# Causal convolution moved to TensorE, second scan direction prepared beside the first rows, local branch added up in DRAM

## The reference

```python
xn = rmsnorm(x)                                   # over channels
u, z = split(xn @ in_proj.T)
u = silu(causal_conv4(u) + conv1d_b)              # depthwise, 4 taps, per direction
dt, Bm, Cm = split(u @ x_proj.T)
delta = softplus(dt @ dt_proj.T + dt_proj_b)
h = exp(delta * A) * h + (delta * u) * Bm         # scan over 1024 tokens, 16 states
y = sum_n(h * Cm) + u * D
mamba = (y * silu(z)) @ out_proj.T
x1 = x + res_scale * (scale_mod * (mamba(xn) + flip(mamba(flip(xn))))
                      + sigmoid(conv3x3(xn) + dw_b) * xn)
x2 = x1 + attention(layernorm(x1))                # 6 heads of 64, causal
out = x2 + mlp(layernorm(x2))                     # 384 -> 1536 -> 384, gelu
```

## Time and profile before

| what | us |
|---|---|
| median of 3 runs | 4690.36 (4688.07 to 4693.26) |
| profiled execution | 4690.52 |
| its span | 4688.3 |
| VectorE busy | 4013.4 (86%) |
| TensorE busy | 3251.8 (69%) |
| POOL busy | 2847.9 (61%) |
| ACT busy | 2447.6 (52%) |

### The profile page before, as it was taken

How to read it: one execution, slowest core, us unless ns; L and a number is a source line. 1 busy time by engine, 2 the same in 40 slices (tenths; PEclk the granted TensorE clock), 3 DMA queues, 4 the chain that set the end, 5 groups by cost and what they waited for, 6 DMA issues and landing times.

```text
span 4688.3 us, 38816 instructions
## 1 busy us (share of the span) xinstructions
PE 3251.8 (69%) x10858; PEld 1667.3 (36%) x10858; DVE 4013.4 (86%) x2961; ACT 2447.6 (52%) x3430; POOL 2847.9 (61%) x1671
## 2 busy tenths in 40 slices
PE   4100677767777768777677777877687776777797
PEld 1000235512354224532255223542245322552372
DVE  5999899989898999989999898988989899998221
ACT  3433446555464555655466544656556554665262
POOL 2798467764676647765577646766477655776100
PEclk8555778877888878878788778888788877888898
DMA  2799469982788639885599828886388855988100
GB/s 85 181 248 246 103 144 206 216 210 77 186 197 216 163 101 207 201 216 131 133 207 207 211 80 188 199 217 167 98 200 200 216 147 123 206 201 186 51 6 14
DMA packets 223126, 772.34 MB, mean 165 GB/s; under 512 B 24666, under 2 KB 40330, under 8 KB 222890
## 3 DMA queue, kind: packets, MB, share of 16 engines
q0 software_dynamic: 110592, 402.70, 44.2%
q1 hardware_dynamic: 112298, 366.90, 24.4%
...
## 4 chain that ended last, share of the span: by engine, by line
DVE 33%; PE 23%; issue 22%; POOL 8%; ACT 8%; DMA 5%; DVEq 1%; SPq 0%; ACTq 0%; POOLq 0%
DVE pBC L1055 16%; POOL hb L1213 7%; PE pW L482 5%; DMA y<-hb 5%; PE pW L421 4%; PE pW L449 4%; DVE stat L1095 3%; PE pW L561 2%; DVE hb L1064 2%; DVE du_f L1008 2%; ACT pBC L716 1%; PE pW L586 1%; ACT area L865 1%; ACT L867 1%; DVE du_f L1162 1%
## 5 line engine op out<-in xcount | busy, mean ns | idle before, releaser
L1055 DVE TENSOR_TENSOR_SCAN pBC<-pBC,hb 128x1024 f32<-128x1024 f32 x768 | 1756.6, 2287 | 90.0 <-ACT pBC L716 53.9
L1224 POOL DMA_DIRECT2D y<-hb x768 | 722.8, 941 | 912.9 <-DVE hb L1064 844.6
L1213 POOL TENSOR_TENSOR hb<-du_f,b_row 128x1024 f32<-128x1024 f32 x384 | 1039.8, 2720 | 61.2 <-DVE du_f L993 48.6
L1213 POOL TENSOR_TENSOR hb<-uc_b,b_row 128x1024 f32<-128x1024 f32 x384 | 1000.1, 2605 | 48.6 <-DMA y<-hb 34.4
L1064 DVE TENSOR_TENSOR hb<-pBC,c_row 128x1024 f32<-128x1024 f32 x768 | 940.6, 1225 | 46.7 <-DVE pBC L1055 3.2
L716 ACT ACTIVATE pBC<-xres,vec 128x1024 f32<-128x1024 f32 x384 | 427.1, 1117 | 337.2 <-DVE hb L1064 336.3
L561 PE MATMUL pW<-area,pt 128*128 128x64 f32 x3456 | 446.4, 284 | 157.9 <-ACT pt L831 157.9
L716 ACT ACTIVATE pBC<-delta,vec 128x1024 f32<-128x1024 f32 x384 | 427.5, 1116 | 198.8 <-DVE hb L1064 198.7
L449 PE MATMUL pW<-area,consts 128*128 128x512 f32 x288 | 162.3, 723 | 487.0 <-ACT area L876 356.3
L561 PEld LDWEIGHTS pW<-area,pt 128*128 128x128 f32 x3456 | 417.5, 198 | 215.6 <-ACT pt L831 207.3
L1095 DVE TENSOR_REDUCE stat<-pW 128x1 f32<-128x640 f32 (+7 forms) x361 | 257.5, 750 | 166.5 <-PE pW L485 166.4
...
## 6 DMA issues: line engine op xcount, KB each, us to landing
y<-hb POOLq DMA_DIRECT2D x768, 512.0 KB, 7.0
b_row<-bc_rows SPq DMA_DIRECT2D x256, 512.0 KB, 5.8
c_row<-bc_rows SPq DMA_DIRECT2D x256, 512.0 KB, 5.0
area<-in_x SPq DMA_DIRECT2D x8, 1536.0 KB, 15.2
xres<-in_x SPq DMA_DIRECT2D x8, 1536.0 KB, 6.3
kept_residual<-xres SPq DMA_DIRECT2D x8, 1536.0 KB, 5.6
xres<-kept_residual SPq DMA_DIRECT2D x8, 1536.0 KB, 11.9
out_x<-xa SPq DMA_DIRECT2D x8, 1536.0 KB, 7.1
```

The lines of the kernel that those rows point to most:

```text
L1055: dve.tensor_tensor_scan(flow(d, buf), flow(d, buf), flow(d, hb[r % NHB][:, :]), 0.0, ALU.mult, ALU.add).then_inc(scan_done, 1)
L1213: pool.tensor_tensor(hb[r % NHB][:, :], du[d][:, k, :], b_row[g % 2][:, :], ALU.mult)\
L1224: pool.dma_start(y[:, k, :], hb[r % NHB][:, :], accum_op=ALU.add).then_inc(y_in[k], 16)
```

## The change

It consists of these parts.
- The 4-tap causal convolution is a chain of four matmuls per half tile with diagonal weights: POOL builds 128 x 128 diagonal matrices `cd` from the taps (3 instructions per sample, in row 84, into the weight buffers `v_w` and `w_ko`), PE multiplies them with four shifted windows of `up`, ACT applies bias and SiLU from PSUM. Direction 0 is done at the boundary, direction 1 together with the z half of the input projection beside rows 0 to 7.
- The items of direction 1 have fixed rows (`STEPS`): z copies in rows 0 to 2, convolution and SiLU in 4 and 7, narrow copies in 9, Abs/Exp/Relu in 9 to 11, logarithms in 12, skip terms in 12 to 14, sums in 14 to 16, products du in 19, 21 and 23, these on POOL. All else starts at row 11 (`R0`). `APART` keeps some pairs in different rows; `mlp_split` is an item of its own.
- SiLU of z is done after the rows, in place (`silu_z`).
- The output projection of sample b - 1 goes right behind the input projection, before the convolution, through two banks, in the next iteration.
- The bias of delta is a 25th row of the `dt` matmul; Abs and Relu have none, and for direction 0 maximum and sum are one VectorE instruction.
- The skip terms are made by ACT: direction 0 into `y`, direction 1 into three buffers of `hb`, which count as three more rows of the ring (behind row 14) and are added to `y` by DMA.
- The residual lies in DRAM: SP copies x to `kept[b]`, POOL adds the gates by accumulating DMA; `xres` is loaded from there at the end.
- SP: weights `q`, `k`, `v` are loaded later, behind the convolutions that use their buffers.

```diff
+R0 = 11
+RS = 15
+STEPS = ([("step_z", n, n) for n in range(3)] + [("step_u", 0, 4), ("step_u", 1, 7), ("step_bc", 0, 9)]
+         + [("step_in", k, 9 + k) for k in range(KT)] + [("step_log", 0, 12)]
+         + [("step_skip", k, 12 + k) for k in range(KT)] + [("step_sum", k, 14 + k) for k in range(KT)]
+         + [("step_du", k, 19 + 2 * k) for k in range(KT)])
+APART = {("ln_var", 0): ("ln_mean", 0), ("ln_var", 1): ("ln_mean", 1), ("scores", 0): ("proj", NPJ - 1),
+         ("mlp_split", 0): ("mlp_in", 0), ("next_square", 0): ("mlp_out", 1)}
...
         def out_bank(t):
-            return pBC[t // 2][:, t % 2 * HALF:(t % 2 + 1) * HALF] if t < 4 else pW[:, t - 4, :]
+            return pW[:, 2 + t % 2, :]
...
+                    sp.dma_start(kept[b], x[b]).then_inc(kept_set, 16)
...
+            def causal(b, d):
+                pe.wait_ge(cd_ready, (3 if b == 0 else 3 * b) if isinstance(b, int) else at(3, b, 0))
+                for i in range(6):
+                    m, c = i // 2, i % 2
+                    if d == 0 and i < 2:
+                        pe.wait_ge(xa_ready, at(6, b, i - 1))
+                    if i < 4:
+                        pe.wait_ge(ip_evac, at(12, b, 6 * d + 3 + i))
+                    elif d == 0:
+                        pe.wait_ge(uc_ready, at(6, b, i - 3))
+                    else:
+                        pe.wait_ge(uc1_raw, at(2, b, i - 3))
+                    for j in range(NTAP):
+                        off = (j if d == 0 else 2 * (NTAP - 1) - j) + c * HALF
+                        mm = pe.matmul(pW[:, (i + 2 - 2 * d) % 4, :], cd[m][:, 128 * j:128 * j + 128],
+                                       up[:, m, off:off + HALF], start=(j == 0), stop=(j == NTAP - 1))
+                    mm.then_inc(cv_ready, 1)
...
+            def out_project(b, lo, hi):
+                for t in range(lo, hi):
...
+                    if t >= 2:
+                        pe.wait_ge(xa_ready, at(6, b, t - 1))
+                    project(out_bank(t), op_w, slice(128 * m, 128 * m + 128), y,
+                            slice(c * HALF, (c + 1) * HALF), op_ready)
...
+                    if layer1:
+                        pe.wait_ge(ip_evac, at(12, b, 4))
+                        out_project(b - 1, 0, 6)
+                    causal(b, 0)
+                    steps_in(b, 0)
+                    for k in range(KT):
+                        step_size(b, 0, k)
+                    in_project(b, 1)
+                    causal(b, 1)
+                    steps_in(b, 1)
...
+            def skip(b, d, k):
+                dcol = vec[:, k, V_D:V_D + 1]
+                if d == 0:
...
+                    act.activation(y[:, k, :], uc[0][:, k, :], ACT.Identity, scale=dcol).then_inc(yd_ready, 1)
+                else:
...
+                    act.wait_ge(y_in[(RS + k - NHB) % KT], at(YIN, b, 16 * ((RS + k - NHB) // KT + 1)))
+                    act.activation(hb[(RS + k) % NHB][:, :], uc[1][:, k, :], ACT.Identity, scale=dcol).then_inc(yd_ready, 1)
...
             def soft_sum(b, d, k):
-                dve.wait_ge(relu_done, at(6, b, 3 * d + k + 1))
                 dve.wait_ge(sp_ready, at(6, b, 3 * d + k + 1))
-                dve.tensor_tensor(delta[d][:, k, :], delta[d][:, k, :], soft[d][k][:, :], ALU.add)\
-                   .then_inc(delta_ready, 1)
...
                 if d == 0:
-                    dve.wait_ge(m1_done, at(ROWS, b, 0))
-                    dve.wait_ge(xres_ready, at(3, b, 3))
+                    dve.wait_ge(da_ready, at(ROWS, b, 0))
+                    dve.scalar_tensor_tensor(out=delta[0][:, k, :], in0=dt_bank[k][:, :], scalar=0.0,
+                                             in1=soft[0][k][:, :], op0=ALU.max, op1=ALU.add).then_inc(delta_ready, 1)
...
+            def times_u(b, k):
+                dve.wait_ge(delta_ready, at(6, b, k + 1))
+                dve.wait_ge(m1_done, at(ROWS, b, 0))
+                dve.wait_ge(kept_add[k], at(16, b, 16))
+                dve.tensor_tensor(du[0][:, k, :], delta[0][:, k, :], uc[0][:, k, :], ALU.mult).then_inc(du_ready, 1)
...
+                elif kind == "step_du":
+                    pool.wait_ge(delta_ready, at(6, b, 4 + n))
+                    pool.wait_ge(yd_ready, at(6, b, 6))
+                    pool.tensor_tensor(du[1][:, n, :], delta[1][:, n, :], uc[1][:, n, :], ALU.mult).then_inc(du_ready, 1)
+
+            def row_of(q):
+                return q if q < RS else q - KT if q >= RS + KT else None
...
+                        pool.dma_start(kept[b][128 * k:128 * k + 128, :], gate[:, k, :], accum_op=ALU.add)\
+                            .then_inc(kept_add[k], 16)
```

359 lines of the change are left out of this document (184 added, 175 removed).

## The result

The changed kernel took 4756.25 us (median of four, 4747.97 to 4765.06) beside 4691.4 us for the kernel before: ratio 1.014, 95% interval 1.0128 to 1.0152. It is slower by 1.4%, where the forecast was 4675 us, 0.3% faster. The time lies inside the stated range (4580 to 4775 us), but on the other side of the kernel before. The profiled execution took 4765.06 us with a span of 4763.3 us, 75.0 us longer than that of before.

The account below looks back on a forecast made before the run. VectorE was taken to set the time almost everywhere. Six middle samples +2, the last -4 and the first -14 gave -16 us on 4690.52: 4675 us, range 4580 to 4775.

Parts of the forecast that it names:

- the sums of direction 1: Rows 14 to 16: VectorE's sums counted at 1.2 us each on top of a 3.47 us row.
- the rest of the rows: Rows after scan 23: same work in a denser table; scores +3.8, split -4, next norm +3.5, GELUs and diagonals +3, together +6.3 us.
- Boundary, -18.4: Between two samples: PE and ACT chain brings the first scan at 1140.2 instead of 1158.65, gaining 18.4 us.
- Ten taps beside six additions: Boundary: ten VectorE taps beside six POOL additions take 12.7 + 9.3 = 22 us, ending long before the sigmoids.
- Direction 1 up to row 13: Early rows: convolution, x projection, Relu and norm make scans late one after another; scan 13 at 70.3 us.
- Row 15, 5.1 for POOL's product: Row 15 waits for the buffer of row 13 through DMA and POOL's product, 10 us in all: 5.1 us late.
- du on POOL, 5.4: Rows 19, 21, 23: three POOL products of 2.98 us make rows 5.4 us late, including the memset of row 22.
- Sample 0, -14: First sample: first scan 29 us sooner, its rows 15 us longer, together -14 us.
- The last sample, -4: Last sample, without steps for a next one: -18.4 + 12.5 + 1.8 = -4 us.
- the first (waits that cover each other): Rival: waits in the rows overlap, 12 us per sample go, 4590 us; under 45 us of waits per sample; chance 0.23.
- The second: Rival: direction 1's convolution in the rows runs at PE's lower clock, 13 us more per sample, 4780 us; chance 0.17.
- The third: Rival: residual's accumulating DMAs to DRAM land one after another, scan 2 is 15 us late, 4795 us; chance 0.10.

Follow-up runs that it names:

- a_sum14: Changed kernel with the three sums of direction 1 all in row 14 instead of rows 14, 15 and 16: 4713.28 us, ratio 1.0042.

## Why the prediction was wrong

Two steps of the sum failed: the sums of direction 1, put at the 1.2 us that each has alone, of which the last takes 8.63 us; and the rest of the rows, put at +6.3 us, which measured +13.2. Every other step of a middle sample is within 3.5 us. A middle sample was to be 0.4 us longer and is 12.1 us longer (549.2 and 561.3). Taken step by step:

- *Boundary, -18.4: measured -16.8.* On the clock of the trace before (the input projection starts at 1054.01 there and at 1049.54 after, so 4.47 is added) the output projection ends at 1089.1 (forecast 1089.3), the convolution at 1109.9 (1110.5), the x projection at 1116.1 (1116.7), the sigmoids at 1122.4 (1123.0), the logarithms at 1132.2 (1133.3), POOL's first row product starts at 1135.2 (1135.7). Every step is within 1.2 us. The first scan is at 1142.1 and was forecast for 1140.2: the term that was too small is the last, 4.4 us from POOL's first product to the scan. It measured 6.9, because VectorE's second and third product stand beside POOL's and take 6.55 us.
- *Ten taps beside six additions, 22 us: measured 22.5.*
- *Direction 1 up to row 13: scan 13 at 70.3, measured 70.0.* Scans 9, 10 and 11 are 1.4, 2.4 and 2.3 us late (0.5, 2.9 and 2.5), the mean 8.4 + 0.8 (7.9 + 1.4), the norm 2.1 (3.1).
- *Row 15, 5.1 for POOL's product: measured 3.4*; scan 15 comes 81.6 us after the first, 1.9 us sooner than the 83.5 of the forecast.
- *The three sums of direction 1.* This is the first step that failed. The prediction let the sums run beside POOL at the 1.2 us that they have alone ("3.47 + 1.2 of work"). They take 1.22, 2.23 and 8.63 us. Rows 15 to 17 in sample 2 take 17.7 us where 2 x (3.47 + 1.2) = 9.3 stood: +8.4. With the steps around it that came sooner than forecast, 3.0 of them are left at scan 23.
- *du on POOL, 5.4: measured 1.7 in one wait of row 23.* Rows 17 to 23 in sample 2 take 22.7 us where 26.2 stood. This was not wrong about POOL but paid under another name: POOL worked off its products while VectorE's sum stood still, and when the sum was moved (`a_sum14`) the lateness came back.
- *Rest of the rows, +6.3 beyond the 5.6 that only move: measured +18.8 where 11.9 stood.* This is the second. Against the earlier trace rows the waits for scores grow by 8.6 (10.8 to 19.4; forecast +3.8), those for decays behind row 11 by 4.9 (4.9 to 9.8; +3), the one for the next norm by 4.6 (0.2 to 4.8; +3.5), and the split gives 6.8 (9.2 to 2.4; -4). Each has its sign right; the first two were sized too low. The prediction counted 8 pairs of neighbouring groups of scores before and 12 after; before they are 9. So fewer new pairs cost more than twice the price. The runs with the table alone show that a few rows there are worth 98 us.
- *Sample 0, -14: measured -13.0.*
- *The last sample, -4:* its boundary, rows and tail are -17.9 + 29.7 + 6.2 = +18.0. Of the 22 us missed 0.5 are in the boundary, 5.1 up to scan 23, 10.2 behind it (rows 26 to 69 take 15.5 us more), and 6.2 in the attention pass behind the rows, which the sum put at nothing. Where those 6.2 arise was not traced.

By these sizes a middle sample misses by 1.6 + 3.0 + 6.9 = 11.5 us. The six together, each with the boundary in front of it, miss 68 of the 91 us between forecast and span, the last sample 22, the first one. With the sums alone moved the kernel is still slower than before (4713.28 us). With the du products moved too, which the forecast had priced, it stands at 4683.67 us, a difference from the kernel before that can't be told from none: so two thirds of the loss against it hang on the sums, the rest on the sums and POOL's du products together.

The prediction did weigh the rule that decided. It cited the Trainium skill, "SBUF — State Buffer", section "Who interferes with whom", at the taps, and set it aside since the taps fitted a softer reading. There the difference was 1 us. In row 16 it is 7.4 us per sample, and there the trace agrees with the lock and goes beyond it: the page speaks of one instruction shut out by one other, as the sum of row 15 was (2.23 us), while the sum of row 16 completes 1.1 us behind the last of three products. The error was to test a rule where it changes nothing and then to leave it out where POOL's queue is full.

Of the rivals, the first (waits that cover each other) is refuted by 66 us of waits in a sample's rows where it wanted under 45. The second is refuted by direction 1's convolution, which ends 27.7 us after the first scan (forecast 28.4), its last tile at the upper clock (granted 1.00 from 1150 to 1172):

```profile
1158.25 7.03 PE L481 MATMUL pW<-area,w_ko 128*128 128x512 f32 x16
```

Scan 9 waits 1.4 us for its decay and scan 10 waits 2.4, where this rival wanted over 10. The third is refuted in size: the second product waits 0.54 us and the third 0.1 us for the residual's DMA, although such a DMA takes 12.2 us to land here, about the 11.9 that this rival took. But the three do not follow one another: issued at 1117.9, 1118.8 and 1120.0, they land at 1127.9, 1131.0 and 1134.2, while POOL's products hold VectorE up as well:

```profile
kept_residual<-du_f POOLq DMA_DIRECT2D x24, 512.0 KB, 12.2
```

All three were about a wait; the part of the loss that no rival had is an instruction that runs long. The signs that the prediction set for itself could not catch it either: the boundary shrank by 16.6 us (12 to 25 allowed), the first scan came 84.9 us after the last multiply (83) with VectorE idle for 25.5 (27), and the waits in the rows were mostly the forecast ones. All these signs watched the boundary and the waits, none an instruction's own length.
